# Unread bf16 matmuls in five waits of TensorE, in a kernel of sparse and local attention on one core

## The chip, the cores and the metric

The kernel runs on one core of a Trainium2 chip. The time is that of one execution on the device, in microseconds (us). The kernel before took 1639.14 us (median of 3 runs, 1638.55 to 1643.65). The core has a matmul engine (PE), a vector engine (DVE), a scalar engine with activation tables (ACT), a general engine (POOL) and a queue that starts DMA transfers (SP). They run side by side and wait for each other on semaphores. PE's clock has two levels, 1.2 and 2.4 GHz; the profile shows the granted share of full speed, 0.50 or 1.00, and averages between them for a stretch that holds both.

## The reference

The input x is 4 batches of 512 tokens of 128 values. Cut to what matters:

```python
xn = layernorm(x)
# a gating net: two layers of windowed attention and feed-forward, on xn
for l in range(2):
    h = shift_token(x); q, k, v = heads(h @ wqkv)          # 8 heads of 64
    q, k = rotary_xpos(l2norm(q) * qs, l2norm(k) * ks)
    x = x + local_attention(q, k, v) @ wo                  # windows of 64, one look back
    h = layernorm(shift_token(x)) * lg + lb
    h = h @ w1 + b1; a, g = split(h); x = x + (a * gelu(g)) @ w2 + b2
# sparse attention on xn: of each query 64 local keys and the 32 best others, by an index score
idx = top_k(sum_h relu(q_i . k_i) * idx_w, 96)
scores = (q_c . key_c[idx] + q_r . key_r[idx]) * scale; s = softmax(scores) @ value[idx] @ W_out
out = x + s * silu(gating net)
```

## The kernel before

One loop (L1592) runs over the four batches. Each turn has three programs, with a barrier of all engines between them: project (L284), latents (L816) and attend (L1077). In each program every engine has its own list of instructions, in the order in which the code is written; nothing is reordered, and an instruction that waits holds up all that is behind it on its engine. PE's results go to eight banks of its output memory, grouped as the regions X, Y, Z (two banks each), W and U (one each). A small class (Region, L149) keeps for each region which semaphore says that its last result has been read: its method start makes PE wait for that before the region is written again.

**Project.** DVE computes the layernorm of the batch into xn (four tiles, L652). PE waits for these (xn_ready), transposes them (L348), ACT copies the result to xnT, and PE multiplies it for the index keys and queries (L353, L356), and those with each other for the index scores (L366), which ACT takes out with a relu. Then come the two layers of the gating net. In each, the attention ends with the output projection (L445); DVE adds the residual (x1, L793) and shifts the tokens (hT, L689 and L690). PE centres them (L485), ACT squares, PE averages the squares (L488), ACT takes a logarithm and an exponential of it, DVE multiplies to hn (L803), and PE does the up matmuls (L493, L496), with GELU on ACT and a product on DVE behind each pair, and the down matmuls (L500), to which DVE adds the residual (x2, L811). In f32 each of these matmuls of 512 columns stands as two instructions in the trace.

**Latents.** PE's last work is turn_ranks (L887), whose results ACT, DVE and POOL split into three bf16 parts each; DVE ends the program with the local queries (L1055, L1058).

**Attend.** DVE makes one-hot matrices of the chosen indices (L1358), PE gathers with them (L1129 and L1135, bf16), ACT and DVE copy the gathered keys, and PE computes scores for one tile of 128 queries after the other. A tile's softmax (jnormed) is used one tile later: PE transposes the probabilities (probs_T, L1171), weighs the values (L1181, L1186), projects (L1196) and turns back (L1202). The fourth and last tile has no tile behind it: DVE normalises it (L1450) and PE waits for that.

What the change touches is PE's list in these three programs: before the transposes L348, before L485, between L488 and L493, behind the last L887, and before the last tile's L1171. The functions follow, with the line numbers of the profile.

Of the kernel before, what the change touches and what calls it, by code (L numbers as in the profile page):

```python
# [20 lines left out]
P = 128  # L21
TILES = L // P
# [259 lines left out]


def project(nc, b, k, scope):  # L284

    F, U32 = mybir.dt.float32, mybir.dt.uint32
    ALU, ACT, AX = mybir.AluOpType, mybir.ActivationFunctionType, mybir.AxisListType
    a, C, W = k.sems, k.C, k.W
# [51 lines left out]
    with nc.Block() as block:  # L340
        @block.tensor
        def _(pe):
            mm = nc.tensor.matmul

            rZ.start(pe, "xnT", a.xnT_ready, 1)
            pe.wait_ge(a.xn_ready, TILES)
            for i in range(TILES):
# [101 lines left out]
            for l in range(LAYERS):  # L449
# [32 lines left out]

                rX.start(pe, f"centred{l}", a.hn_ready, l + 1)
                pe.wait_ge(a.hT_ready, 2 * l + 2)
                mm(k.X[:, 0, :], C("centre"), hT[:, WIN:], start=True, stop=True).then_inc(rX.full, 1)  # L485
                rY.start(pe, f"var{l}", a.lnh_ready, l + 1)
                pe.wait_ge(a.sqh_ready, l + 1)
                mm(k.Y[:, 0, :], C("mean_ones"), sq[:, 0, :], start=True, stop=True).then_inc(rY.full, 1)  # L488
                pe.wait_ge(a.hn_ready, l + 1)
                for j, (off, n) in enumerate(HCH):  # L490
# [5 lines left out]
                    mm(reg[0:n, 1, :], W("w1", l * 2 * HID + off, n), hn, start=True, stop=True).then_inc(r.full, 1)  # L496
                rU.start(pe, f"down{l}", a.x2_ready, l + 1)
                for j, (off, n) in enumerate(HCH):
# [317 lines left out]
def latents(nc, b, k, scope):  # L816
# [3 lines left out]
    a, C, W = k.sems, k.C, k.W  # L820
# [56 lines left out]
    with nc.Block() as block:  # L877
        @block.tensor
        def _(pe):
# [33 lines left out]
            for j in range(1, TILES):  # L913
                turn_ranks(j)

        @block.scalar
# [160 lines left out]
def attend(nc, b, k, scope):  # L1077
# [39 lines left out]
    with nc.Block() as block:  # L1117
        @block.tensor
        def _(pe):
# [47 lines left out]
            def probs_T(i):  # L1167
                rX.start(pe, f"lt{i}", a.jpT_ready, i + 1)
                pe.wait_ge(a.jnormed, i + 1)
                for h in range(HEADS):  # L1170
                    last = nc.tensor.transpose(k.X[:, h // 4, (h % 4) * P:(h % 4 + 1) * P], SC[:, i % 2, h, 0:SLOTS], C("ident"))  # L1171
                last.then_inc(rX.full, 1)
# [284 lines left out]
def build(nc, x_d, const_d, rot_d, weights_d, setup_d, scratch, q_scratch, out_d):  # L1457
# [4 lines left out]
    with top:  # L1462
# [18 lines left out]
        def C(name, rows=P):  # L1481
            return consts[0:rows, cc.at[name][0]:cc.at[name][1]]
# [103 lines left out]
        k.sb, k.C, k.W, k.PS, k.X, k.Y, k.Z, k.Wb, k.Ub = sb, C, W, PS, X, Y, Z, Wb, Ub  # L1586
        k.x_next, k.C2, k.soft_kr = x_next, C2, soft_kr
        k.x_in, k.xnT, k.gate, k.idx_h, k.m1, k.mo, k.rot_tab = x_in, xnT, gate, idx_h, m1, mo, rot_tab
        k.x_d, k.out_d, k.scratch, k.q_scratch = x_d, out_d, scratch, q_scratch
# [88 lines left out]
```

## Time and profile before

| what | value |
|---|---|
| median of 3 runs | 1639.14 us |
| the profiled execution | 1635.37 us, its span 1633.7 us |
| granted clock of PE, mean | 0.828 |
| PE busy | 1154.4 us (71%), 8816 matmul instructions |
| DVE busy | 992.6 us (61%), 1835 instructions |
| ACT busy | 623.1 us (38%), 1381 instructions |
| POOL busy | 251.6 us (15%) |
| DMA packets' share of 16 engines | 17.8% on the data queue |

The span goes from the first to the last instruction; the execution has 1.7 us around it. A busy share is an average over the whole span. Which engine sets the pace changes from one stretch to the next, and is read from the waits of that stretch. A busy time of PE holds the modelled ends of pipelined matmuls: the distance from one start to the next tells what one matmul costs in a dense row. The records of the granted clock begin some 55 us into the span; ahead of that the profile shows 1.00, and the level is read from the matmuls' durations.

### The profile page before, as it was taken

How to read it: one execution, taken by the hardware profiler on the slowest of the kernel's cores; microseconds unless marked ns; L12 is line 12 of the kernel's file. 1: busy time of each engine (PE TensorE's matmuls, PEld its weight loads, DVE VectorE, ACT ScalarE, POOL GpSimd, SP SyncE). 2: the span in 40 equal slices, each digit the busy share in tenths (PEclk: the TensorE clock that was granted, in tenths of full speed). 3: DMA queues.
4: the chain of work that ended last, by engine and by line, in shares of the span. 5: the costliest groups of instructions: out<-in, count | busy, mean ns of one | idle time of the engine just before them, and what ended most of it. 6: DMA issues, size and time to landing. Idle time of an engine off the chain costs nothing. (4 is left out here: it accounts for less than half of the span.)

```text
span 1633.7 us, 22979 instructions
## 1 busy us (share of the span) xinstructions
PE 1154.4 (71%) x8816; PEld 755.5 (46%) x8816; DVE 992.6 (61%) x1835; ACT 623.1 (38%) x1381; POOL 251.6 (15%) x172
## 2 busy tenths in 40 slices
PE   2777876578497777569749687756856868684785
PEld 2454542456255354146526445325643545532563
DVE  2575856676356574767527567386842948637773
ACT  0352445233225354524322525543332442553332
POOL 0320302001122131101012122120001302111000
PEclk9998975789689898579959889857977989866897
DMA  5000001553000000165200000026410000005530
GB/s 212 1 1 1 1 1 52 94 78 48 5 1 1 1 1 15 39 110 77 32 5 1 1 0 2 14 71 98 72 19 4 1 1 1 1 14 106 90 55 10
DMA packets 231276, 54.51 MB, mean 33 GB/s; under 512 B 220048, under 2 KB 230800, under 8 KB 230800
## 3 DMA queue, kind: packets, MB, share of 16 engines
q1 hardware_dynamic: 231152, 52.86, 17.8%
q8 instruction: 78, 1.28, 0.3%
q14 instruction: 46, 0.38, 0.1%
HBM read 45.37 MB, written 7.47 MB: 32 GB/s over the span
## 5 line engine op out<-in xcount | busy, mean ns | idle before, releaser
L1129 PE MATMUL PS<-onehot,CX 128*96 128x512 bf16 x320 | 91.9, 422 | 93.5 <-DVE onehot L1358 90.6
L1381 DVE TENSOR_REDUCE xnT<-PS 32x64 f32<-32x192 f32 x256 | 90.8, 355 | 69.2 <-ACT V L1307 65.6
L579 ACT ACTIVATE S<-S,nbias,rnorm 128x128 f32<-128x128 f32 x256 | 122.3, 479 | 25.8 <-DVE nbias L735 25.8
L1299 ACT ACTIVATE KC<-PS 96x1024 bf16<-96x1024 f32 x64 | 65.1, 1018 | 126.2 <-PE PS L1129 126.2
L1358 DVE TENSOR_SCALAR onehot<-idxb,consts 128x1024 bf16<-128x1024 f16 x160 | 77.6, 537 | 52.9 <-DMA idxb<-idx_scratch 48.7
L566 ACT ACTIVATE sq<-PS 128x512 f32<-128x512 f32 x64 | 38.2, 597 | 178.1 <-PE PS L376 178.1
L1135 PEld LDWEIGHTS PS<-onehot,XR 128*96 128x96 bf16 x1280 | 87.5, 134 | 25.6 <-DVE KR L1364 16.1
L1129 PEld LDWEIGHTS PS<-onehot,CX 128*96 128x96 bf16 x320 | 36.9, 132 | 126.6 <-DVE onehot L1358 101.5
L700 DVE SCALAR_TENSOR_TENSOR pb<-PS,wts,consts 128x512 f32<-128x512 f32 x64 | 48.0, 750 | 77.0 <-PE PS L376 75.1
L1135 PE MATMUL PS<-onehot,XR 128*96 128x128 bf16 x1280 | 92.1, 232 | 3.2 <-DVE KR L1364 2.9
L1364 DVE CAST KR<-PS 96x1024 bf16<-96x1024 f32 x64 | 78.1, 1220 | 26.7 <-PE PS L1135 25.7
L1289 POOL TENSOR_TENSOR SC<-SC,jrec 128x1280 f32<-128x1280 f32 x12 | 27.9, 2322 | 376.9 <-DVE jrec L1396 376.9
L531 POOL TENSOR_TENSOR S<-S,rrec 128x1024 f32<-128x1024 f32 x32 | 61.1, 1908 | 148.8 <-DVE rrec L741 148.8
L375 PE MATMUL PS<-hT,wts 128*128 128x512 f32 x128 | 72.5, 649 | 16.0 <-DVE pa L703 8.9
L1313 ACT ACTIVATE SC<-SC,jbias 128x160 f32<-128x160 f32 x128 | 52.9, 414 | 78.4 <-DVE jbias L1392 78.4
L528 POOL TENSOR_TENSOR ab<-pa,pb 128x512 f32<-128x512 f32 x32 | 40.8, 1276 | 272.2 <-DVE pa L703 272.2
L389 PEld LDWEIGHTS PS<-consts,sq 128*128 128x128 f32 x512 | 68.7, 197 | 28.7 <-issue 28.7
L424 PE MATMUL PS<-consts,S 128*128 128x128 f32 x256 | 42.6, 320 | 43.5 <-ACT pT L591 28.9
L1163 PE MATMUL PS<-q3c,KC 96*128 96x128 bf16 x512 | 63.5, 228 | 11.8 <-ACT PT L1319 8.9
L1146 PE MATMUL PS<-key,q_loc 128*64 128x128 f32 x512 | 42.2, 334 | 40.5 <-DVE xnT L1381 40.5
L406 PE MATMUL PS<-wts,hT 128*128 128x512 f32 x128 | 62.7, 612 | 10.3 <-DVE v L746 10.3
L376 PE MATMUL PS<-hT,wts 128*128 128x512 f32 x128 | 68.5, 618 | 0.0
(218 smaller groups left out, 2649.9 us busy)
## 6 DMA issues: line engine op xcount, KB each, us to landing
idxb<-idx_scratch SPq DMA_DIRECT2D x64, 256.0 KB, 4.9
q3c<-q_scratch SPq DMA_DIRECT2D x96, 96.0 KB, 3.0
q3r<-q_scratch SPq DMA_DIRECT2D x96, 96.0 KB, 3.8
q_scratch<-q3s SPq DMA_DIRECT2D x16, 384.0 KB, 2.5
wts<-weights_dram SPq DMA_DIRECT2D x1, 4825.5 KB, 20.6
consts<-consts_dram SPq DMA_DIRECT2D x1, 2612.5 KB, 9.0
x_next<-x_dram SPq DMA_DIRECT2D x5, 256.0 KB, 6.5
out<-soft_kr SPq DMA_DIRECT2D x16, 64.0 KB, 1.7
```

Of the source, the lines that this page charges most:

```text
L375: mm(reg[:, 0, :], W("qkv", l * 3 * INNER + which * INNER + c * P, P), hT[:, WIN:], start=True, stop=True)
L376: mm(reg[:, 1, :], W("rot", l * 2 * INNER + which * INNER + c * P, P), hT[:, WIN:], start=True, stop=True).then_inc(r.full, 1)
L389: last = mm(reg[:, at:at + 2], sq[:, n % 2, tile(i)], C("pair_ones"), start=True, stop=True)
L406: last = mm(k.Z[:, par, :], hT[:, at:at + P], W("qkv", l * 3 * INNER + 2 * INNER, INNER), start=True, stop=True)
L579: last = op(S[:, i, h, :], S[:, i, h, :], ACT.Exp, bias=nbias[:, i, h:h + 1], scale=rnorm[:, Q, h // 2, i, h % 2:h % 2 + 1], accum_out=rsu ...
L1129: last = mm(k.Z[0:96, e, :], k.CX[:, j, :], onehot[:, n % 2, j, e * 512:(e + 1) * 512], start=(j == 0), stop=(j == i))
L1135: last = mm(k.Y[0:96, r // 4, (r % 4) * P:(r % 4 + 1) * P], k.XR[:, j, q * RB + r, :], onehot[:, n % 2, j, r * P:(r + 1) * P], start=(j == ...
L1163: mm(out, KC[:, i % 2, t, :], q3c[:, :, GR * t:GR * t + GR], start=True, stop=False)
L1299: op(KC[:, i % 2, :, :].rearrange("p t (g r) -> p t g r", g=GR)[:, :, :, q * RB:(q + 1) * RB], k.Z[0:96, :, :].rearrange("p a (r g t) -> p ...
L1358: last = ve.tensor_scalar(onehot[:, n % 2, j, :], idxb[:, n % 2, :], C("iota")[:, j:j + 1], None, ALU.is_equal)
L1364: ve.tensor_copy(KR[:, i % 2, :, :].rearrange("p t (g r) -> p t g r", g=GR)[:, :, :, q * RB:(q + 1) * RB], k.Y[0:96, :, :].rearrange("p a ...
L1381: last = ve.tensor_reduce(SN[32 * g:32 * g + 32, :, 8 * o:8 * o + 8].rearrange("p h t -> p t h"), part, AX.X, ALU.add)
```

## The change

A new function spin issues a matmul again and again: 128 x 128 bf16 weights and 512 bf16 columns, both taken from the bytes of two f32 constants (mean_ones, centre), into one bank. Nothing reads the result, and no semaphore is raised. It is called in five places: 13 times at the start of each batch, into the second bank of Z; in each layer 9 times ahead of the wait for the shifted tokens, into the second bank of X, and 14 times ahead of the wait for hn, into U; 40 times at the end of latents, into U; 25 times ahead of the wait for the last tile's probabilities, into the first bank of X. That is 13 + 2 x 23 + 40 + 25 = 124 in a batch and 496 in all. For the 14 into U, the wait for U's last reader (x1) moves from the down matmuls to ahead of the 14.

```diff
@@ -281,6 +281,12 @@
     pass
 
 
+def spin(nc, k, bank, count):
+
+    for _ in range(count):
+        nc.tensor.matmul(bank, k.spin_w, k.spin_x, start=True, stop=True)
+
+
 def project(nc, b, k, scope):
 
     F, U32 = mybir.dt.float32, mybir.dt.uint32
@@ -343,6 +349,7 @@
             mm = nc.tensor.matmul
 
             rZ.start(pe, "xnT", a.xnT_ready, 1)
+            spin(nc, k, k.Z[:, 1, :], 13)
             pe.wait_ge(a.xn_ready, TILES)
             for i in range(TILES):
                 last = nc.tensor.transpose(k.Z[:, 0, tile(i)], xn[:, i, :], C("ident"))
@@ -481,11 +488,14 @@
                 project_heads(l, TILES - 1)
 
                 rX.start(pe, f"centred{l}", a.hn_ready, l + 1)
+                spin(nc, k, k.X[:, 1, :], 9)
                 pe.wait_ge(a.hT_ready, 2 * l + 2)
                 mm(k.X[:, 0, :], C("centre"), hT[:, WIN:], start=True, stop=True).then_inc(rX.full, 1)
                 rY.start(pe, f"var{l}", a.lnh_ready, l + 1)
                 pe.wait_ge(a.sqh_ready, l + 1)
                 mm(k.Y[:, 0, :], C("mean_ones"), sq[:, 0, :], start=True, stop=True).then_inc(rY.full, 1)
+                rU.start(pe, f"down{l}", a.x2_ready, l + 1)
+                spin(nc, k, k.Ub, 14)
                 pe.wait_ge(a.hn_ready, l + 1)
                 for j, (off, n) in enumerate(HCH):
                     reg, r = pair(j)
@@ -494,7 +504,6 @@
                        start=True, stop=True).then_inc(r.full, 1)
                     r.more(f"up{l}.{j} linear")
                     mm(reg[0:n, 1, :], W("w1", l * 2 * HID + off, n), hn, start=True, stop=True).then_inc(r.full, 1)
-                rU.start(pe, f"down{l}", a.x2_ready, l + 1)
                 for j, (off, n) in enumerate(HCH):
                     pe.wait_ge(a.hid_ready, 3 * l + j + 1)
                     last = mm(k.Ub, W("w2", (l * 3 + j) * D, D, rows=n), hid[0:n, j, :], start=(j == 0), stop=(j == 2))
@@ -912,6 +921,8 @@
             mm(k.Wb, k.m1[:, P:2 * P], cqT[:, :], start=True, stop=True).then_inc(rW.full, 1)
             for j in range(1, TILES):
                 turn_ranks(j)
+            rU.start(pe, "idle", a.qc_ready, 1)
+            spin(nc, k, k.Ub, 40)
 
         @block.scalar
         def _(act):
@@ -1166,6 +1177,8 @@
 
             def probs_T(i):
                 rX.start(pe, f"lt{i}", a.jpT_ready, i + 1)
+                if i == TILES - 1:
+                    spin(nc, k, k.X[:, 0, :], 25)
                 pe.wait_ge(a.jnormed, i + 1)
                 for h in range(HEADS):
                     last = nc.tensor.transpose(k.X[:, h // 4, (h % 4) * P:(h % 4 + 1) * P], SC[:, i % 2, h, 0:SLOTS], C("ident"))
@@ -1585,6 +1598,8 @@
         k = Core()
         k.sb, k.C, k.W, k.PS, k.X, k.Y, k.Z, k.Wb, k.Ub = sb, C, W, PS, X, Y, Z, Wb, Ub
         k.x_next, k.C2, k.soft_kr = x_next, C2, soft_kr
+        k.spin_w = C("mean_ones").bitcast(BF)[:, 0:P]
+        k.spin_x = consts[:, cc.at["mean_ones"][0]:cc.at["centre"][1]].bitcast(BF)
         k.x_in, k.xnT, k.gate, k.idx_h, k.m1, k.mo, k.rot_tab = x_in, xnT, gate, idx_h, m1, mo, rot_tab
         k.x_d, k.out_d, k.scratch, k.q_scratch = x_d, out_d, scratch, q_scratch
         k.sems = Signals(sem)
```

PE's list at the start of a batch, before (the rows are line, instruction, output and inputs by name, size of the output, and the semaphores that it waits for; pT holds xn):

```order
L341 UNCONDITIONAL_BRANCH
L348 MATMUL PS<-consts,pT 128x128 [waits xn_ready]
L348 MATMUL PS<-consts,pT 128x128 x3
L353 MATMUL PS<-xnT,wts 128x512 [waits xnT_ready]
L356 MATMUL PS<-xnT,wts 128x512 x2
L366 MATMUL PS<-kiZ,qiT 128x64 [waits qi_ready,ki_ready,zeroed]
```

and after; the 13 stand between the loop's branch and the first transpose, which alone waits for xn_ready:

```order
L347 UNCONDITIONAL_BRANCH
L287 MATMUL PS<-consts 128x512 x13
L355 MATMUL PS<-consts,pT 128x128 [waits xn_ready]
L355 MATMUL PS<-consts,pT 128x128 x3
L360 MATMUL PS<-xnT,wts 128x512 [waits xnT_ready]
L363 MATMUL PS<-xnT,wts 128x512 x2
L373 MATMUL PS<-kiZ,qiT 128x64 [waits qi_ready,ki_ready,zeroed]
```

Nothing else has moved there; the lines of what follows are 7 higher.

PE's list in the feed-forward block of the first layer, before (S is the memory that holds hn and the product of GELU, hT the shifted tokens, sq the squares):

```order
L445 MATMUL PS<-oT,wts 128x128 [waits o_ready]
L445 MATMUL PS<-oT,wts 128x128 x3
L485 MATMUL PS<-hT,consts 128x512 [waits hT_ready,masked_ready]
L488 MATMUL PS<-sq,consts 128x512 [waits sqh_ready,masked_ready]
L493 MATMUL PS<-S,wts 128x512 [waits hn_ready]
L496 MATMUL PS<-S,wts 128x512
L493 MATMUL PS<-S,wts 128x512 [waits lnh_ready]
L496 MATMUL PS<-S,wts 128x512
L493 MATMUL PS<-S,wts 85x512 [waits hid_ready]
L496 MATMUL PS<-S,wts 85x512
L500 MATMUL PS<-S,wts 128x512 [waits hid_ready,x1_ready]
L500 MATMUL PS<-S,wts 128x512 [waits hid_ready] x2
```

and after:

```order
L452 MATMUL PS<-oT,wts 128x128 x3
L287 MATMUL PS<-consts 128x512 [waits masked_ready]
L287 MATMUL PS<-consts 128x512 x8
L493 MATMUL PS<-hT,consts 128x512 [waits hT_ready]
L496 MATMUL PS<-sq,consts 128x512 [waits sqh_ready,masked_ready]
L287 MATMUL PS<-consts 128x512 [waits x1_ready]
L287 MATMUL PS<-consts 128x512 x13
L503 MATMUL PS<-S,wts 128x512 [waits hn_ready]
L506 MATMUL PS<-S,wts 128x512
L503 MATMUL PS<-S,wts 128x512 [waits lnh_ready]
L506 MATMUL PS<-S,wts 128x512
L503 MATMUL PS<-S,wts 85x512 [waits hid_ready]
```

The 9 stand between the output projection (L445, now L452) and the centring matmul (L485, now L493), the 14 between the averaging matmul (L488, now L496) and the first up matmul (L493, now L503). The wait for x1_ready, which was at the first down matmul, is at the first of the 14; the wait of the 9, for masked_ready, was at the centring matmul.

PE's list at the last tile of attend, before (SC holds the probabilities, soft_kr the gathered output):

```order
L1196 MATMUL PS<-soft_kr,mo 128x128 [waits oT_ready]
L1196 MATMUL PS<-soft_kr,mo 128x128
L1202 MATMUL PS<-consts,soft_kr 128x128 [waits fT_ready]
L1171 MATMUL PS<-consts,SC 128x128 [waits jnormed,jpT_ready]
L1171 MATMUL PS<-consts,SC 128x128 x7
L1181 MATMUL PS<-PT,ckvS 32x16x16 [waits blocks_ready,jpT_ready,out_ready]
L1181 MATMUL PS<-PT,ckvS 32x16x16
L1186 MATMUL PS<-PB,V 32x32 x16
```

and after:

```order
L1209 MATMUL PS<-soft_kr,mo 128x128 [waits oT_ready]
L1209 MATMUL PS<-soft_kr,mo 128x128
L1215 MATMUL PS<-consts,soft_kr 128x128 [waits fT_ready]
L287 MATMUL PS<-consts 128x512 [waits jpT_ready]
L287 MATMUL PS<-consts 128x512 x24
L1184 MATMUL PS<-consts,SC 128x128 [waits jnormed]
L1184 MATMUL PS<-consts,SC 128x128 x7
L1194 MATMUL PS<-PT,ckvS 32x16x16 [waits blocks_ready,jpT_ready,out_ready]
L1194 MATMUL PS<-PT,ckvS 32x16x16
L1199 MATMUL PS<-PB,V 32x32 x16
```

The 25 stand behind the third tile's last transpose (L1202 before, L1215 after); their first waits until the third tile's transposed probabilities were copied (jpT_ready), and the last tile's transposes wait for jnormed alone.

## Rows read from the trace of the kernel before

**Rows 1.** Which line of the page has the span
```profile
span 1633.7 us, 22979 instructions
```

**Rows 2.** PE's waits: line, awaited instruction, total us, times, longest us
```profile
PE PS L1129 <- DVE onehot L1358: 90.6, 21, 17.0
PE PS L493 <- DVE S L803: 28.6, 8, 3.6
PE PS L1171 <- DVE SC L1450: 17.7, 4, 4.4
PE PS L485 <- DVE hT L690: 14.3, 8, 1.8
```

**Rows 3.** Stretches: us, busy us (instructions) of PE, PEld, DVE, ACT, POOL, clock, DMA, GB/s
```profile
137.00:140.00 3.00, 0.00 (x1) 0.03 (x1) 0.69 (x1) 2.95 (x4) 0.00 (x0) 1.00 0.00 0
255.00:275.00 20.00, 18.63 (x22) 6.30 (x21) 12.99 (x14) 12.96 (x14) 4.90 (x2) 0.50 0.00 0
418.20:422.70 4.50, 0.12 (x1) 0.00 (x0) 2.05 (x4) 2.64 (x14) 0.00 (x0) 0.50 0.05 15
442.80:447.10 4.30, 0.00 (x0) 0.00 (x0) 3.87 (x12) 0.73 (x2) 4.22 (x4) 0.50 0.02 4
532.00:535.00 3.00, 1.18 (x3) 0.30 (x2) 2.68 (x8) 0.00 (x0) 0.00 (x0) 1.00 0.00 0
```

**Rows 4.** Attend's gather, in order of time: start, length, instruction, wait
```profile
293.96 1.09 PE L1129 MATMUL PS<-onehot,CX 128*96 128x512 bf16 x2 [16.99 <-DVE onehot L1358]
294.84 1.06 PE L1135 MATMUL PS<-onehot,XR 128*96 128x128 bf16 x8
...
374.90 1.93 PE L1129 MATMUL PS<-onehot,CX 128*96 128x512 bf16 x8 [0.19 <-DVE onehot L1358]
376.67 1.95 PE L1135 MATMUL PS<-onehot,XR 128*96 128x128 bf16 x32
```

**Rows 5.** The loop's branch at L1592, PE's sequencer; ns and first start
```profile
L1592 PEldq COMPARE_BRANCH  x4: 79/3614/4177, 439.1 to 1633.6; - x4
...
L1592 PEldq MOVE  x1: 29/29/29, 43.6 to 43.6; - x1
```

**Rows 6.** PE in order of time, start of two batches
```profile
47.14 1.11 PE L348 MATMUL PS<-consts,pT 128*128 128x128 f32 x4 [8.94 <-DVE pT L652]
...
55.75 7.92 PE L366 MATMUL PS<-kiZ,qiT 128*128 128x64 f32 x32 [1.32 <-ACT qiT L549]
...
447.12 1.11 PE L348 MATMUL PS<-consts,pT 128*128 128x128 f32 x4 [11.13 <-DVE pT L652]
...
450.79 3.59 PE L356 MATMUL PS<-xnT,wts 128*128 128x512 f32 x4
455.70 9.41 PE L366 MATMUL PS<-kiZ,qiT 128*128 128x64 f32 x32 [1.32 <-ACT qiT L549]
```

**Rows 7.** Feed-forward: two of eight stretches, their sum, passes of 512 columns
```profile
541.00:552.40 11.40, 10.62 (x18) 4.19 (x18) 2.97 (x4) 2.44 (x4) 0.00 (x0) 0.76 0.00 0
635.60:645.80 10.20, 9.40 (x18) 3.78 (x18) 3.00 (x4) 3.74 (x5) 0.00 (x0) 0.86 0.00 0
...
sum 85.10, PE 78.66 PEld 31.08 DVE 23.94 ACT 24.75 POOL 0.00; mean PE 9.83 PEld 3.89 DVE 2.99 ACT 3.09 POOL 0.00
...
146.92 2.74 PE L500 MATMUL PS<-S,wts 128*128 128x512 f32 x6
...
L488 PE MATMUL PS<-sq,consts 128*128 128x512 f32 x16 | 11.8, 830 | 8.6 <-ACT sq L614 8.6
```

**Rows 8.** Transposes and block matmuls of attend's tiles in order of time
```profile
378.45 1.04 PE L1171 MATMUL PS<-consts,SC 128*128 128x128 f32 x8
...
407.74 1.19 PE L1186 MATMUL PS<-PB,V 128*32 128x32 f32 x32
...
422.75 1.94 PE L1171 MATMUL PS<-consts,SC 128*128 128x128 f32 x8 [4.43 <-DVE SC L1450]
...
427.56 1.89 PE L1186 MATMUL PS<-PB,V 128*32 128x32 f32 x32
```

## The prediction

> **What bounds the kernel now.** I read the page first for the span [rows 1], then who waits for whom on PE, then stretches with their granted clock, then the instructions in order of time at the five places where matmuls are added. The span is four batches of about 400 us. In attend the biggest wait of PE, 90.6 us, is for DVE's one-hots [rows 2]: there PE is not the bound and its clock is worth little. It is different at the start of a batch and in the feed-forward block: there PE works nearly alone (10.62 of 11.40 us) on f32 matmuls, behind a wait, at a granted clock that is half for a part of the stretch [rows 6, 7]. The clock has two levels, 1.2 GHz (granted 0.50) and 2.4 GHz (1.00). The waits themselves show what comes before: with PE at rest and ACT busy 2.95 of 3.00 us the clock is still 1.00 before the first feed-forward block, and PE's next matmuls start at half; the waits at the start of a batch and in the last tile (one row of four that read alike) stand at 0.50 [rows 3].
>
> **What one added matmul costs.** Its nearest row is the bf16 matmul of 512 columns in attend. At the high level eight of them start at 374.90 and the next group at 376.67: 0.22 us each. At the low level two start at 293.96 and the next group at 294.84: 0.44 us each [rows 4]. Busy ends hold a modelled tail of some 0.16 us (eight transposes 1.04 us at 0.11 [rows 8]), so a wait can take 0.16 us more than its row says. How long dense work stays at the low level before the clock rises is read from the eight feed-forward stretches: twice the missing clock times the length gives 2 x 0.24 x 11.4 = 5.5 us in the worst and 2 x 0.14 x 10.2 = 2.9 us in the best; the other six lie between, mean 3.8 us [rows 7]. I take 3.8 us.
>
> **Start of a batch (13).** PE comes back from the loop's branch at 439.1 + 3.6 = 442.7 and waits until 447.12: 4.4 us; in the first batch from 43.6 to 47.14, 3.5 us; where the branch took its longest, 4.18 us, about 3.8 us [rows 5, 6]. At 3.8 us of low level, 8.6 matmuls are done and 4.4 remain at 0.22: 4.8 us. Overrun 0.4, 0.4, 1.0 and 1.3 us: 3.1 us in four batches. Bounds: 2.9 us (all high, no overrun) and 5.7 us (all low, 6.8 us in all). What it gives back: four transposes 1.11 -> 0.6 us; four f32 passes take 3.59 us [rows 6], 0.85 each, against six in 2.74 us at the high level, 0.43 each [rows 7], so the six between transposes and index scores save 2.5 us; these lie on the path, since ACT and DVE wait for them and PE waits for ACT 1.32 us, which stays. The index scores took 7.92 us in the first and last batch and 9.41 us in the two between [rows 6]; there 1.5 us go. Together 4.5, 4.5, 3.0 and 3.0 = 15.0 us, less 3.1: **-11.9 us**.
>
> **Feed-forward, first wait (9).** PE waits 14.3/8 = 1.8 us for the shifted tokens [rows 2], plus 0.16. The clock there is high in all eight cases (one row stands [rows 3]). 9 x 0.22 = 1.98 us against 1.95: nothing to 0.1 us late each, **+0.4 us** for eight.
>
> **Feed-forward, second wait (14).** 28.6/8 = 3.6 us [rows 2] while ACT does a logarithm, an exponential and table loads, and DVE one multiply. If the first nine keep the clock up through the wait before it, 14 x 0.22 = 3.1 us fits with 0.6 us to spare. Then the eighteen passes of up and down run at 0.43: 7.7 us + 0.16 tail + 0.8 for the residual add = 8.7 us. GELU and the gated product don't take over: DVE is busy 2.97 and ACT 2.44 us of 11.40 [rows 7]. The eight stretches last 85.1 us [rows 7] against 8 x 8.7 = 69.6: -15.5 us. The variance matmul L488 holds 11.8 us in eight pairs, a high pair 1.1 us, so -3.0 us, all on the chain to hn [rows 7]. **-18.5 us.** Bounds: if every added matmul runs at 0.44 and the clock afterwards too, 6.2 against 3.75 us: +2.4 each, +19.6. If it falls in the last 0.6 us, half the gain. The wait for x1 that is moved ahead of these was met long before (x1 is what the first wait is for).
>
> **End of latents (40).** PE has nothing to do from 277 to 293.96, 16.99 us [rows 2, 4]. At 3.8 us low and the rest high the 40 take 3.8 + 31.4 x 0.22 = 10.7 us and end at 287.7. DVE's chain, which ends the program, hides them. Then 6 us of rest follow, twice the idle stretch behind which the feed-forward's matmuls began at half [rows 3], so I let the fetches again start low: **0**. Bounds: -1 us a batch if the clock holds (estimate: half of the first fetch, two matmuls at 0.44 and eight shorter ones; the next fetches wait for DVE); all low, 17.6 us, +0.6 us, and up to 2 us (estimate) with the barrier and the one-hots that now lie inside the wait.
>
> **Last tile (25).** The wait is 4.43 us, + 0.16, and begins at the low level in this and the three other batches [rows 2, 3, 8]. 25 take 3.8 + 16.4 x 0.22 = 7.4 us, so the transposes that the tile's end hangs on start 2.8 us late, and behind them queue PT's copy on ACT, the weighing, the last two projections and the store. Back come eight transposes 1.94 -> 1.04 us and the first 32 block matmuls 1.89 -> 1.19 us [rows 8]; the second 32 were high before. Net **+1.2 us** a batch, **+4.8 us**. Bounds: with 2.9 us at low +0.8, with 5.5 us +2.1, never rising +6.4 a batch; all high -0.7.
> The Trainium skill, page "TensorE: Matmul & The Clock Gate", section "Part 4: PE-mode transpose", says that transposes do not count as work for the clock. That speaks against this place: behind the 25 stand only transposes and the wait for PT's copy; by it the block matmuls could be low again and the term +1.9 instead of +1.2 us a batch. No row here decides it.
>
> **Sum.** -11.9 + 0.4 - 18.5 + 0 + 4.8 = -25.2 us. The profiled execution took 1635.37 us (span 1633.7 and 1.7 around it), which gives 1610; the median of the runs is 1639.14, 3.8 us above it, so I predict 1614 us. PE's added 496 matmuls are otherwise in nobody's way: their banks are waited free (the semaphores were met long before) and no other queue is touched.
>
> **Rivals.**
> Half the gain: the clock falls again in the short waits behind the fillers (0.6 us before hn, 1.32 us at the start), as it falls in longer ones now. Half of 18.5, about 6 of 11.9, loss of 5.2 kept: -10 us, 1629. For it: the index scores of two batches lost 1.5 us right behind such short waits [rows 6]. Against: the waits left are shorter than the idle stretch of [rows 3].
> No change: the stretches are bound by something that PE's clock doesn't move, gains and overruns cancel: 1639. Against: PE is busy 10.62 of 11.40 us in the stretch.
> Slower: the constant matmuls do not raise the clock. For it stands a stretch of latents, 255 to 275, where PE works 18.63 of 20.00 us and is granted 0.50 throughout [rows 3]; these matmuls contract over 32 or 64 rows of the array. Against: attend's bf16 matmuls over 128 rows, the nearest kind, stand at 0.44 us at attend's start and at 0.22 later in it [rows 4]. Price: start 6.8, second feed-forward wait 19.6, latents 2 to 8, last tile 4 x 6.4 = 25.6: some 57 us, 1696. It decides once fillers stand at 0.44 us throughout and the matmuls behind them at 0.85; the last tile alone then costs more than the start could give.
> The Trainium skill, same page, section "What's actually happening", has the low level as the default and PE's activity as what lifts it. By that rule without more the sum above stands; the latents stretch shows a busy PE at the low level, so by this row it would be 1696 us.
>
> **How the numbers follow.** Forecast 0.75, half the gain 0.12, no change 0.06, slower 0.07. The forecast's own range: the low stretch of 2.9 or 5.5 us instead of 3.8 moves start and last tile by -4 to +7 us, latents by -4 to 0, and stretches that I don't touch will meet the clock's level at other moments (feed-forward stretches that do the same work differ by 1.2 us, index scores by 1.5), say 5 us: 1604 to 1624. Eight in ten reaches up to the half gain: 1603 to 1631. What this kernel's measurement can tell from no change is about 0.3%, 5 us. Faster by more: 0.87; within: 0.06; slower: 0.07.
>
> **What would show it.** Right: the eight feed-forward stretches at granted clock 1.00 and near 8.7 us; index scores 7.9 us in all batches; PE's first transposes 0.4 to 1.3 us later against DVE's last normalised tile; in the last tile the 25 ending about 2.8 us after DVE's multiply; the latents' fillers ending near 10.7 us with the first fetch still at 0.44. Wrong: fillers at 0.44 to their end; up matmuls still at 0.85 behind the 14; a hn wait that becomes a wait for PE itself; or the weighing no sooner, which would make the last tile's loss the full 2.8 us.

## The result, and the profile after

The changed kernel took 1620.09 us (median of 4 runs, 1614.79 to 1621.74), the kernel before 1638.85 us beside it (4 runs, 1630.84 to 1643.65). The ratio is 0.9885, with a 95% interval from 0.9839 to 0.9931: faster by 1.15%. The forecast was 1614 us, 0.4% below, with a range of 1603 to 1631. The profiled execution went from 1635.37 to 1621.74 us, 13.6 us less, where the forecast's sum had 25.2. The table cuts both profiled executions at the same instructions; each number is a sum over four batches, read from the rows in order of time. Each column is one execution. Executions of the kernel before lie up to 13 us apart (1630.84 to 1643.65), so a difference of 2 or 3 us in a stretch can be such variation. The cut at x1 is the start of its add, the cut at x2 the end.

| stretch | before | after | difference | forecast |
|---|---|---|---|---|
| load, layernorm, to the last xn | 79.2 | 80.0 | +0.8 | 0 |
| last xn to the first query matmul (13) | 68.6 | 57.8 | -10.8 | -11.9 |
| attention, first layer | 270.5 | 268.4 | -2.1 | 0 |
| x1 to x2, both layers (9 and 14) | 156.9 | 138.7 | -18.2 | -18.1 |
| attention, second layer | 299.7 | 302.5 | +2.9 | 0 |
| x2 to the first ranks (opening of latents) | 30.8 | 44.0 | **+13.2** | 0 |
| ranks to the first fetch (40) | 160.6 | 160.8 | +0.2 | 0 |
| first fetch to the last tile's normalisation | 510.0 | 502.9 | **-7.1** | 0 |
| last normalisation to the end (25) | 54.7 | 62.1 | +7.4 | +4.8 |

The stretches with fillers came out near their forecast (their sum is -21.4 against -25.2 us). What the forecast did not have at all is the opening of latents, where no instruction was added, and attend, where the fillers of the last tile are not yet reached. The +13.2 us is far above the variation and stands in all four batches (10.8 to 11.1 us against 7.6 to 7.8).

The page of the changed kernel has the span, 13.7 us below that of [rows 1]:

```profile
span 1620.0 us, 23951 instructions
```

PE's waits after answer to [rows 2]; the lines of attend stand 11 to 13 higher, those of project 10 higher at hn. Columns are the awaited instruction, total us, times, longest us:

```profile
PE PS L1140 <- DVE onehot L1371: 48.3, 21, 7.1
PE PS L1184 <- POOL SC L1302: 15.1, 4, 3.8
PE PS L901 <- PEq L1610: 8.3, 4, 2.1
PE PS L503 <- DVE S L812: 4.5, 8, 0.6
```

In the kernel before, the second of these rows was:

```profile
PE PS L1171 <- POOL SC L1289: 15.1, 4, 3.8
```

The wait for hn fell from 28.6 to 4.5 us and the waits for one-hots from 90.6 to 48.3, because PE is busy in them. That alone says nothing of time: what counts is when the next matmul starts and how long it takes. The 15.1 us of L1184 are the wait for the third tile, which POOL normalises, and have not changed. The last tile's wait for DVE, 17.7 us in [rows 2], is gone from the list, since the 25 end behind DVE's multiply. The row of L901 is the barrier between project and latents, 2.1 us of rest for PE in each batch; it will matter.

**Feed-forward.** In the changed kernel, in order of time (start, length, instruction, wait):

```profile
526.56 2.11 PE L287 MATMUL PS<-consts 128*128 128x512 bf16 x9
...
531.26 3.18 PE L287 MATMUL PS<-consts 128*128 128x512 bf16 x14
535.06 1.10 PE L503 MATMUL PS<-S,wts 128*128 128x512 f32 x2 [0.62 <-DVE S L812]
```

The 9 end as hT arrives, the 14 leave 0.62 us, and the clock stays up through both. Windows from the first up matmul to x2 answer to [rows 7] (the first of eight that read alike, and their sum; columns as in [rows 3]):

```profile
139.30:148.05 8.75, 7.96 (x18) 3.16 (x18) 3.00 (x4) 2.41 (x4) 0.00 (x0) 1.00 0.01 2
...
sum 70.06, PE 63.72 PEld 25.32 DVE 24.00 ACT 24.75 POOL 0.00; mean PE 7.96 PEld 3.16 DVE 3.00 ACT 3.09 POOL 0.00
```

All eight last 8.75 or 8.76 us at granted clock 1.00, where before they lasted 10.2 to 11.4 us; the sum fell from 85.10 to 70.06 us.

**Start, latents' end and last tile.** The same view at the other three places; the start answers to [rows 6], the fetch to [rows 4], the last tile to [rows 8]:

```profile
275.36 10.09 PE L287 MATMUL PS<-consts 128*128 128x512 bf16 x40
292.48 1.09 PE L1140 MATMUL PS<-onehot,CX 128*96 128x512 bf16 x2 [7.03 <-DVE onehot L1371]
...
413.00 8.01 PE L287 MATMUL PS<-consts 128*128 128x512 bf16 x25
420.85 1.04 PE L1184 MATMUL PS<-consts,SC 128*128 128x128 f32 x8
...
424.75 1.89 PE L1199 MATMUL PS<-PB,V 128*32 128x32 f32 x32
426.45 1.90 PE L1194 MATMUL PS<-PT,ckvS 128*32 128x256 f32 x4
...
431.06 0.69 PE L1209 MATMUL PS<-soft_kr,mo 128*128 128x128 f32 x4 [1.70 <-ACT soft_kr L1338]
...
439.29 5.73 PE L287 MATMUL PS<-consts 128*128 128x512 bf16 x13 [6.61 <-issue]
444.81 0.82 PE L355 MATMUL PS<-consts,pT 128*128 128x128 f32 x4
...
447.28 1.88 PE L363 MATMUL PS<-xnT,wts 128*128 128x512 f32 x4
450.51 9.41 PE L373 MATMUL PS<-kiZ,qiT 128*128 128x64 f32 x32 [1.35 <-ACT qiT L558]
```

At the start of this batch the last xn was ready at 443.76, so the transposes are 1.05 us late; the other three batches were 1.83, 0.06 and 0.05 us late. The four passes of L363 fell from 3.59 to 1.88 us, but the index scores of this batch still took 9.41 us. In the last tile DVE's multiply ended at 417.49 (row below), so the transposes start 3.36 us late.

```profile
415.99 1.49 DVE L1463 TENSOR_TENSOR SC<-SC,jrec 128x1280 f32<-128x1280 f32 x1
```

**The opening of latents.** PE's first matmuls behind the barrier in the changed kernel, and its window from x2 to the first ranks in the first batch (the other three read alike, 10.82 to 11.13 us):

```profile
242.60 1.04 PE L901 MATMUL PS<-xnT,wts 128*64 128x512 f32 x2 [2.09 <-PEq L1610]
243.57 1.81 PE L902 MATMUL PS<-xnT,wts 128*128 128x512 f32 x2
245.18 3.46 PE L907 MATMUL PS<-wts,xnT 128*128 128x32 f32 x16
```

```profile
241.30:252.28 10.98, 9.68 (x25) 5.32 (x25) 1.74 (x4) 2.59 (x5) 4.51 (x3) 0.62 0.20 48
```

The same window of the kernel before (the others 7.58 to 7.84 us):

```profile
246.23:253.82 7.59, 6.15 (x25) 3.11 (x25) 1.74 (x4) 2.59 (x5) 4.63 (x3) 0.93 0.31 71
```

Two of its rows, the 16 matmuls of L907 above and the last ones ahead of the ranks:

```profile
249.47 1.87 PE L898 MATMUL PS<-wts,xnT 128*128 128x32 f32 x16
...
252.41 1.48 PE L906 MATMUL PS<-cqT,wts 64*128 64x512 f32 x2
```

The same 25 instructions take 3.4 us longer at a granted clock of 0.62 instead of 0.93. DVE, ACT and POOL do the same work in both. PE's rest in front is 2.09 us long in both.

### The profile page after: what moved, and what is told of

It reads as the page before. It is cut to its first block and busy times, and to the rows that moved or that the text cites. A ratio compares the mean times of both kernels' runs of the same rounds, so it can differ in the third digit from the quotient of the medians.

```text
span 1620.0 us, 23951 instructions
## 1 busy us (share of the span) xinstructions
PE 1262.5 (78%) x9312; PEld 802.6 (50%) x9312; DVE 991.4 (61%) x1835; ACT 623.0 (38%) x1381; POOL 251.1 (15%) x172
## 5 line engine op out<-in xcount | busy, mean ns | idle before, releaser
L287 PE MATMUL PS<-consts 128*128 128x512 bf16 x496 | 136.2, 438 | 25.2 <-issue 19.7
L1140 PE MATMUL PS<-onehot,CX 128*96 128x512 bf16 x320 | 89.7, 414 | 51.6 <-DVE onehot L1371 48.3
L287 PEld LDWEIGHTS PS<-consts 128*128 128x128 bf16 x496 | 53.9, 110 | 107.2 <-issue 68.2
L382 PE MATMUL PS<-hT,wts 128*128 128x512 f32 x128 | 73.5, 657 | 14.4 <-DVE pa L712 7.4
L1326 ACT ACTIVATE SC<-SC,jbias 128x160 f32<-128x160 f32 x128 | 52.9, 414 | 76.1 <-DVE jbias L1405 76.1
L537 POOL TENSOR_TENSOR ab<-pa,pb 128x512 f32<-128x512 f32 x32 | 40.8, 1277 | 248.2 <-DVE pa L712 248.2
L1174 PE MATMUL PS<-q3c,KC 96*128 96x128 bf16 x512 | 64.3, 230 | 11.1 <-ACT PT L1332 8.9
L383 PE MATMUL PS<-hT,wts 128*128 128x512 f32 x128 | 71.9, 646 | 0.0
```

Source lines behind the costliest of these rows:

```text
L287: nc.tensor.matmul(bank, k.spin_w, k.spin_x, start=True, stop=True)
L382: mm(reg[:, 0, :], W("qkv", l * 3 * INNER + which * INNER + c * P, P), hT[:, WIN:], start=True, stop=True)
L383: mm(reg[:, 1, :], W("rot", l * 2 * INNER + which * INNER + c * P, P), hT[:, WIN:], start=True, stop=True).then_inc(r.full, 1)
L1140: last = mm(k.Z[0:96, e, :], k.CX[:, j, :], onehot[:, n % 2, j, e * 512:(e + 1) * 512], start=(j == 0), stop=(j == i))
L1174: mm(out, KC[:, i % 2, t, :], q3c[:, :, GR * t:GR * t + GR], start=True, stop=False)
```

## The experiments

The theory after the result: fillers raise PE's clock and keep it up over a short wait, each place has its own price, and what the sum missed is the clock's level at places that were not touched. The main rivals: the fillers help or cost in another way than by the clock; and what a place gains or loses is handed on to the next, so that single places can't be priced. Each ratio is against runs of the kernel before on the same chip. The first four leave in one place's fillers and take out the others (diffs against the changed kernel).

**Feed-forward alone.**

```diff
-            spin(nc, k, k.Z[:, 1, :], 13)
...
-            rU.start(pe, "idle", a.qc_ready, 1)
-            spin(nc, k, k.Ub, 40)
...
-                if i == TILES - 1:
-                    spin(nc, k, k.X[:, 0, :], 25)
```

> Of the five places only the two in the feed-forward blocks (9 and 14). Theory (fillers hold PE's clock up behind their wait): the eight stretches from x1 to x2 go from 156.9 to 138.7 us in all as in the changed kernel, up stretches at granted clock 1.00 and 8.75 us; 18 us faster than before, 1621, give or take 5 for stretches that are not touched. Rival (the changed kernel's gain comes from where the clock's falls land in the whole program, not from the fillers): the stretches don't all stand at 1.00, or the total is off by more than 8 us.

Measured 1626.46 us, ratio 0.9948 [0.9931, 0.9966]: 10.5 us below the kernel before beside it (1636.98), where 18 were expected. x1 to x2 lost the same 18.2 us as in the changed kernel, with all eight windows at 8.75 or 8.76 us. But the opening of latents got 6.6 us longer, and attend 2.5. The window of the opening (one of four, 9.34 to 9.37 us):

```profile
241.29:250.64 9.35, 7.92 (x25) 3.56 (x25) 1.74 (x3) 2.60 (x5) 4.51 (x3) 0.74 0.24 56
```

So part of the missed 13.2 us follows from the feed-forward's own fillers, in a stretch behind them that they don't touch.

**Start alone.**

```diff
-                spin(nc, k, k.X[:, 1, :], 9)
...
-                spin(nc, k, k.Ub, 14)
...
-            rU.start(pe, "idle", a.qc_ready, 1)
-            spin(nc, k, k.Ub, 40)
...
-                if i == TILES - 1:
-                    spin(nc, k, k.X[:, 0, :], 25)
```

> Only the 13 at the start of each batch. Theory: from DVE's last normalised tile to the first qk matmul 13.3 to 16.0 us in place of 16.4 to 17.9, with the first transpose 0.1 to 1.8 us late: 8 to 13 us faster, 1627 to 1631. Rival (what the early matmuls gain the next stretch gives back, because ACT and DVE set its pace): 1639, with the qk stretch longer by what the start gained.

Measured 1634.85 us, ratio 0.9990 [0.9971, 1.0010]: no change that can be told. The start itself got 7.8 us shorter. The feed-forward stretches gave 4.6 us back (x1 to x2); the sum of their eight windows, 85.10 us in [rows 7], is 86.45 us here. In the profiled executions 2.3 of the 7.8 us are left: most of what the start gains is given back by stretches behind it, with nothing changed in them. The rival had the time right, but not the place: the stretch of the query and key matmuls right behind the start, which ACT and DVE were to hold, is 0.5 us shorter.

**Last tile alone.**

```diff
-            spin(nc, k, k.Z[:, 1, :], 13)
...
-                spin(nc, k, k.X[:, 1, :], 9)
...
-                spin(nc, k, k.Ub, 14)
...
-            rU.start(pe, "idle", a.qc_ready, 1)
-            spin(nc, k, k.Ub, 40)
```

> Only the 25 in the last tile. Theory: the tile's end, from DVE's multiply to the store, takes 15.5 us in place of 13.7 as in the changed kernel: 7 us slower than before, 1646. Rival (the 25 pay by a clock that stays up into the next batch's start): as fast as before or faster, with the index scores or transposes of the next batch at the high level.

Measured 1647.53 us, ratio 1.0073 [1.0050, 1.0096]: the 25 cost time. The end got 7.9 us longer, as in the changed kernel. Yet the starts of the next three batches got 6.25 us shorter in sum, with no filler in them, and attention and feed-forward got 8.0 us longer, with none either. The second batch:

```profile
449.76 2.38 PE L362 MATMUL PS<-xnT,wts 128*128 128x512 f32 x4
453.47 7.92 PE L372 MATMUL PS<-kiZ,qiT 128*128 128x64 f32 x32 [1.32 <-ACT qiT L555]
```

In [rows 6] these took 3.59 and 9.41 us. Here the rest before the transposes was 11.13 us, as it was there.

**Latents alone.**

```diff
-            spin(nc, k, k.Z[:, 1, :], 13)
...
-                spin(nc, k, k.X[:, 1, :], 9)
...
-                spin(nc, k, k.Ub, 14)
...
-                if i == TILES - 1:
-                    spin(nc, k, k.X[:, 0, :], 25)
```

> Only the 40 at the end of latents. Theory: they end some 7 us before the first fetch, which starts at the low level as before: within 2 us of before, 1639. Rival (the 40 are what made attend of the first two batches 3 us shorter in the changed kernel): 3 to 7 us faster, with the stretch from the first fetch to the last tile's multiply near 125 us in all four batches in place of 128.6, 128.3, 127.8 and 125.2.

Measured 1638.18 us, ratio 1.0019 [1.0003, 1.0035]. The stretch from ranks to the first fetch kept its length (+0.2 us), attend got 2.75 us longer. The four parts alone, -0.52, -0.10, +0.73 and +0.19%, would make +0.3%; together they made -1.15% (-0.69% at the weak end of the interval). They do not add.

**Narrow fillers.** All 496 stay, but contract over 32 rows instead of 128.

```diff
-        k.spin_w = C("mean_ones").bitcast(BF)[:, 0:P]
-        k.spin_x = consts[:, cc.at["mean_ones"][0]:cc.at["centre"][1]].bitcast(BF)
+        k.spin_w = C("mean_ones", 32).bitcast(BF)[:, 0:P]
+        k.spin_x = consts[0:32, cc.at["mean_ones"][0]:cc.at["centre"][1]].bitcast(BF)
```

> The change with every filler contracting over 32 rows instead of 128 (the fillers only; all that is read stays): same number, same columns. Theory (the gain is PE's clock, and the clock needs wide work): the fillers themselves stand at 0.44 us, the up and down matmuls behind them at 0.85, the stretch x2 less first up is 10.2 us or more instead of 8.75, the 14 run over into hn by some 2.5 us, the last tile's 25 by some 6 us; about 1690 us. Rival (any matmul, however narrow, keeps the clock up, or the gain isn't the clock): fillers at 0.22, stretch 8.75 us, 1620 us.

Measured 1670.95 us (1664.89 to 1687.15), ratio 1.0224 [1.0185, 1.0263]. First layer's 14 and the last tile's 25, in order of time, then the window of the 25 (that of the 14 has 0.50 too), the first batch's window from the second layer's up matmuls to x2, and the sum of the eight feed-forward windows:

```profile
138.58 6.15 PE L287 MATMUL PS<-consts 32*128 32x512 bf16 x14
144.66 2.08 PE L503 MATMUL PS<-S,wts 128*128 128x512 f32 x2
...
421.31 10.84 PE L287 MATMUL PS<-consts 32*128 32x512 bf16 x25
432.08 1.97 PE L1184 MATMUL PS<-consts,SC 128*128 128x128 f32 x8
```

```profile
421.30:432.00 10.70, 10.70 (x26) 3.48 (x25) 3.91 (x8) 2.59 (x14) 0.00 (x0) 0.50 0.02 6
...
239.29:249.53 10.24, 9.45 (x18) 3.81 (x18) 3.00 (x4) 3.78 (x5) 0.00 (x0) 0.85 0.01 2
...
sum 87.20, PE 80.86 PEld 32.26 DVE 23.99 ACT 22.89 POOL 0.00; mean PE 10.11 PEld 4.03 DVE 3.00 ACT 2.86 POOL 0.00
```

PE is busy without a gap and is granted 0.50 for 10.7 us. The 25 end 6.4 us behind DVE's multiply (3.4 with wide ones), and the up matmuls start at half speed. This is the price that the rival "slower" had described, with its cause; it came to 35 us above the kernel before (1635.90 beside it), not 51 to 57. In the second layer the 14 still stood at 0.22 us in three of four batches and ended ahead of hn, but the clock fell all the same right behind them: the window lasts 10.24 us where it is 8.76 with wide fillers and 10.20 without any [rows 7]. So the gain is the clock, and PE's being busy is not enough for it: between these two kernels only the rows that the fillers contract over differ.

**A bridge over the barrier.** The changed kernel and 7 more fillers behind the last layer's down matmuls, into the second bank of X.

```diff
                 last.then_inc(rU.full, 1)
+                if l == LAYERS - 1:
+                    rX.start(pe, "bridge", a.hid_ready, 3 * l + 3)
+                    spin(nc, k, k.X[:, 1, :], 7)
```

> The change plus 7 fillers behind the last layer's down matmuls, into the second bank of X, that lie across the barrier between project and latents (PE rests there some 2.1 us, and behind it its clock was low: x2 to the ranks took 10.8-11.1 us a batch instead of 7.6-7.8). Theory (the rest at the barrier lets the clock fall): x2 to ranks back at 7.3-8.0 us, -12 to -13 us, 1607 us. Rival (the clock falls there for what came before, the narrow latent matmuls follow anyhow): low 2.4 us later or at the same time, 10-11 us as before, 1620 us, or up to 1623 with 7 x 0.22 in the way of the barrier.

Measured 1599.75 us (1596.98 to 1605.72), ratio 0.9793 [0.9773, 0.9814]. In order of time, and the window from x2 to the first ranks:

```profile
240.05 1.68 PE L287 MATMUL PS<-consts 128*128 128x512 bf16 x7
242.36 1.04 PE L904 MATMUL PS<-xnT,wts 128*64 128x512 f32 x2 [0.64 <-PEq L1613]
...
244.30 1.87 PE L910 MATMUL PS<-wts,xnT 128*128 128x32 f32 x16
```

```profile
241.00:248.19 7.19, 6.41 (x29) 3.21 (x27) 1.74 (x4) 2.59 (x5) 4.33 (x3) 1.00 0.32 73
```

PE's rest fell from 2.09 to 0.64 us, the clock stayed at 1.00 to the first ranks in all four batches, and the opening is 7.18 or 7.19 us: 15.2 us less than in the changed kernel, where 12 to 13 were expected. The stretch from ranks to fetch gave 8.0 us more, because the clock now falls among the ranks and not before them (1.00 to 248.2, 0.61 on average from there to 258). So with the rest at the barrier filled, the missed 13.2 us are gone. The rest is not the whole cause: it was 2.09 us long in the kernel before too, whose opening took 30.8 us in sum, against 28.7 with the bridge.

**More fillers at latents' end.**

```diff
-            spin(nc, k, k.Ub, 40)
+            spin(nc, k, k.Ub, 64)
```

> The change with 64 instead of 40 fillers at the end of latents: at 0.22 they end about 16 us after their first instead of 10, 1 us ahead of the first one-hot. Theory of the forecast (the 6 us of rest behind the 40 lets the clock fall, and the first fetch runs at the low level): first fetch at 0.22 instead of 0.44, about -1 us a batch, 1616 us. Rival (attend's first steps wait for DVE's one-hots, so PE's clock is worth nothing there): first fetch quicker, fetch to last normalisation unchanged to 0.5 us a batch, 1620 us.

Measured 1620.90 us, ratio 0.9912 [0.9894, 0.9930]: as the changed kernel. The first fetch does start high, 0.63 us for two instead of 1.09:

```profile
275.07 15.24 PE L287 MATMUL PS<-consts 128*128 128x512 bf16 x64
292.19 0.63 PE L1140 MATMUL PS<-onehot,CX 128*96 128x512 bf16 x2 [1.88 <-DVE onehot L1371]
```

but attend from its first fetch took 504.1 us in sum against 502.9. The rival was right: DVE's one-hots set that pace. This kernel also showed by chance what the bridge shows on purpose. Its third batch, x2 to ranks, lasted 10.94 us at a granted clock of 0.62; its fourth:

```profile
1427.01:1434.12 7.11, 5.68 (x24) 3.10 (x24) 1.73 (x3) 2.59 (x5) 4.32 (x3) 1.00 0.32 74
```

One program, one piece of code: the clock falls in one batch and holds in the next, and 3.8 us hang on it. The rest at the barrier is the same in both.

**Without the last tile's fillers.**

```diff
-                if i == TILES - 1:
-                    spin(nc, k, k.X[:, 0, :], 25)
```

> The change without the 25 at the last tile. Theory (each stretch keeps its own price): jn to end goes from 15.5 back to 13.6-13.7 us a batch, -7.4 us against the changed kernel, 1613 us; start, feed-forward and latents as in the changed kernel. Rival (what is taken out comes back at the next start): with the 25 alone the next batch's start was 2 us quicker each without any filler of its own, 6.25 us in all, so here the starts of batches 2 to 4 get slower by up to 6 us: 1619 us, no change. It is told apart by the time from the last normalised tile to the first query matmul, in batches 2 to 4.

Measured 1613.54 us, ratio 0.9867 [0.9844, 0.9889]. The end fell from 62.1 to 52.9 us in sum, 9.3 less. The start gave 1.1 us back, all of it in the first batch, which has no last tile ahead of it; the starts of batches 2 to 4, which were to tell, took 42.0 us in sum against 42.6. The ratio's interval overlaps that of the changed kernel, so the total alone doesn't settle it. The same edit on the kernel with the bridge does:

> The change plus the 7 across the barrier, without the 25 at the last tile. Theory (the two prices stand apart, each in its own stretch): jn to end back from 15.5 to 13.1-13.7 us a batch, -7.5 us against the kernel with the 7, 1592 us. Rival (single parts do not add: without the 25 the clock is low when the next batch starts, its 13 run over or the index scores are low): -2 us, 1598 us.

Measured 1592.88 us, ratio 0.9736 [0.9712, 0.9759], against 0.9793 [0.9773, 0.9814] with the 25: they cost some 9 us, 7.1 of them in the end of the tile (54.9 us in sum against 61.9).

**Ten instead of 25, on the kernel with the bridge.**

```diff
-                    spin(nc, k, k.X[:, 0, :], 25)
+                    spin(nc, k, k.X[:, 0, :], 10)
```

> The change plus the 7, with 10 instead of 25 at the last tile. At the low level 8.6 matmuls take the 3.8 us after which the clock has risen before, the other 1.4 take 0.3 us: 4.1 us in a wait of 4.6, so no overrun. Theory of the forecast's working (the loss at the last tile is overrun alone; the transposes and block matmuls gain 1.6 us where the clock is up): jn to end 12.1-12.5 us, about 5 us less than without the 25, 1587 us. Rival (10 are too few to raise the clock, or it rises and falls before the block matmuls): 13.0-13.7 us, as without any, 1592 us.

Measured 1588.86 us (6 runs, 1579.27 to 1592.62), ratio 0.9701 [0.9672, 0.9730]: the fastest kernel here. The last tile of the first two batches:

```profile
409.54 4.47 PE L287 MATMUL PS<-consts 128*128 128x512 bf16 x10
414.08 1.69 PE L1187 MATMUL PS<-consts,SC 128*128 128x128 f32 x8
...
418.64 1.83 PE L1202 MATMUL PS<-PB,V 128*32 128x32 f32 x32
...
803.72 1.44 PE L1187 MATMUL PS<-consts,SC 128*128 128x128 f32 x8
...
808.03 1.19 PE L1202 MATMUL PS<-PB,V 128*32 128x32 f32 x32
```

The 10 end in the wait, and the transposes start 0.05 us behind DVE. The clock rises during them and not in the fillers, so the end lasts 11.7 to 12.0 us in three batches, and 12.9 in the first, where the clock fell again before the block matmuls; without any filler it was 13.7. In sum the end takes 48.5 us, against 54.9 without fillers and 61.9 with 25. The intervals of the whole time overlap for 10 and none, so it is this stretch that parts them. The theory of the forecast's working (overrun is the loss) holds.

**Without the 40, on the kernel with the bridge and without the 25.**

```diff
-            rU.start(pe, "idle", a.qc_ready, 1)
-            spin(nc, k, k.Ub, 40)
```

> The change plus the 7, without the 25 and without the 40 at the end of latents. Theory (the first fetch starts at the low level either way, and attend waits for DVE): fetch to last normalisation as with the 40, 125-126.5 us a batch, 1592 us like the kernel with the 40. Rival (the 40 are what took 7 us out of attend's stretch in the changed kernel: 125.7 us with them, 128.1 with the feed-forward's fillers alone): back to 128 us a batch, +7 to +10 us, 1600 us.

Measured 1597.09 us, ratio 0.9767 [0.9746, 0.9787], against 0.9736 [0.9712, 0.9759] with them. The intervals overlap; the medians differ by 4 us. In the profiled executions attend took 505.9 us without and 508.7 us with them, and with the 40 alone attend was not shorter either (+2.75), so nothing here puts attend's 7.1 us in the changed kernel down to the 40.

## Why the prediction was right, and where its sum was off

**What an added matmul costs**, 0.22 or 0.44 us: right. The nearest row was attend's gather, and the fillers stand at these two distances everywhere.

**Start, -11.9 us:** measured -10.8. The low stretch was longer in the first two batches (the 13 took 5.0 and 5.1 us from first to last start) and shorter in the others (3.9 us); the overrun of 3.0 us in sum is near the 3.1 of the forecast, but by luck. The forecast had 0.4 to 1.3 us in every batch; here it was 1.83 and 1.05 us in the first two, where the 13 stood at 0.43 us nearly to their end, and 0.06 or less in the others, where the first six stood at 0.43 and the rest soon at 0.22. The second batch's index scores stayed at 9.41 us, which accounts for the 1.5 us of [rows 6] that did not come, and the sign "7.9 us in all batches" failed there. A pause for ACT lies ahead of them, 1.35 us long.

**Feed-forward, +0.4 and -18.5 us:** measured -18.2 in sum, with 8.75 us where 8.7 was worked out. It rested on the clock at 1.00 ahead of the first wait [rows 3], and on PE being busy 10.62 of 11.40 us [rows 7]; both were read from the stretch itself.

**Latents' end, 0:** right (+0.2), with 10.09 us against 10.7 for the 40, and the first fetch low as assumed. The bound of -1 us a batch was false: with 64 fillers the fetch is quicker and attend no shorter.

**Last tile, +4.8 us:** measured +7.4, the term that was mis-sized. The transposes were 3.3 to 3.5 us late instead of 2.8, and the block matmuls did not come back: the first 32 took 1.89 us as before. The last projections, which the sum left out, gave 0.5 us back: 0.69 us for the four of L1209 above, 1.19 before:

```profile
433.88 1.19 PE L1196 MATMUL PS<-soft_kr,mo 128*128 128x128 f32 x4 [1.70 <-ACT soft_kr L1325]
```

In the first batch the transposes start 3.2 us later against DVE's multiply than before and take 0.9 less, which with the 0.5 makes the measured +1.8. The windows of the changed kernel from the transposes on show the block matmuls' clock:

```profile
420.85:422.00 1.15, 1.03 (x9) 0.79 (x7) 0.00 (x0) 0.08 (x1) 0.00 (x0) 1.00 0.00 0
...
423.04:424.60 1.56, 1.56 (x4) 0.49 (x5) 0.00 (x0) 0.00 (x0) 0.00 (x0) 1.00 0.00 0
424.75:426.40 1.65, 1.65 (x33) 1.65 (x32) 0.00 (x0) 0.00 (x0) 0.00 (x0) 0.51 0.00 0
```

The clock fell behind the transposes, the wait for PT and the four matmuls of L1194. It need not fall there. In the fourth batch of the kernel with the bridge, behind the same 25, the end took 14.7 us instead of 15.6 to 15.8:

```profile
1581.11 1.03 PE L1187 MATMUL PS<-consts,SC 128*128 128x128 f32 x8
...
1585.02 1.19 PE L1202 MATMUL PS<-PB,V 128*32 128x32 f32 x32
```

The Trainium skill, page "TensorE: Matmul & The Clock Gate", section "Part 4: PE-mode transpose", says that transposes don't count as work for the clock. The forecast put +1.9 us a batch beside that rule, and the measured 7.4/4 = 1.85 is near it by luck, since the longer overrun and the projections' gain nearly cancel; behind the same transposes both levels occur, so no run here shows the rule.

**"Stretches that I don't touch": 0, with 5 us in the range.** This is the step that failed in size. Untouched stretches moved by +13.2, -7.1, +2.9, -2.1 and +0.8 us, which is +7.7 in sum. The forecast took in the clock ahead of each place where matmuls were added, and not behind; it had the latents stretch with PE busy and granted 0.50 [rows 3], but did not ask where in the opening the clock falls. Before, it fell in the last matmuls ahead of the ranks (window at 0.93, L906 at 1.48 us for two). Afterwards it fell during the first matmuls behind the barrier (L902 at 1.81 us for two). The bridge shows that this does not happen when PE's rest there is filled; why the same rest did no such harm before stays open.

Attend's -7.1 us is open. 6.3 us of it lie between the first fetch and the first tile's transposes, as these windows of the first batch show, before and then after:

```profile
293.96:347.45 53.49, 37.01 (x370) 28.15 (x371) 34.63 (x61) 18.19 (x34) 4.25 (x3) 0.78 0.64 99
```

```profile
292.48:343.16 50.68, 36.96 (x371) 28.40 (x371) 34.41 (x61) 18.09 (x34) 4.25 (x3) 0.81 0.65 105
```

It is not the level of the first fetch (the 64), and it came with the narrow fillers too (attend 503.0 us). Over the kernels whose windows were read the stretch took 49.7 to 53.9 us for the same instructions, and the whole of attend 125.2 to 128.6 us within the four batches of the kernel before, so a part can be chance. Which of the clock's falls in it decides was not tried.

**The rivals.** The gain by the medians, 18.8 us, lies between the forecast's 25.2 and the 10 of "half the gain" (1629), but not for that rival's reason: the clock did not fall in the short waits behind the 9 and the 14, and what is missing was lost in a stretch that it did not name. Only the index scores of one batch, 1.5 us, fit it. "No change" is outside the interval. "Slower" needed fillers that don't raise the clock; the narrow ones are such, and the kernel with them was slower. Its evidence, a busy PE at 0.50 over few rows of the array, was read rightly and did not apply to 128 rows.

## What to carry to other kernels

Fill a wait of PE only to its end: 10 fillers gained where 25 lost. The number that is safe is the wait over the filler's distance at the low clock (4.6 / 0.43 is 10), since how many run low differed from batch to batch (six, or all 13, at the start). Then follow the clock beyond the place that was filled, to the next rest of PE in front of dense matmuls (here a barrier of 2.1 us, where 7 fillers took 20 us off the median), since a stretch that nobody touched can lose what the filled one gains. Price a set of such edits together, and by stretches: alone these four came to +0.3%, together to -1.15%.

## What the hardware showed that was not expected

- A rest of 2.09 us in front of the same 25 instructions left them at granted clocks from 0.61 to 1.00: 0.91 to 0.93 in the four batches before, 0.73 or 0.74 with the feed-forward's fillers, 0.61 to 0.63 in the changed kernel, and 1.00 in one batch with 64 at latents' end. Within one kernel the four batches mostly agree; what decides between them no run took apart.
- PE without a gap at the low level: 10.70 of 10.70 us busy with matmuls over 32 rows, granted 0.50 throughout.
- These matmuls don't get faster with the clock: four of L1194 (weights of 32 columns, f32) took 1.89 us at 1.00 (423.04) and 1.90 us at 0.50 (426.45).
